# A fused attention and expert layer on one core: alibi transfers issued by GpSimd, a reordered prologue, and the last head's masks, gates and sums moved

## The chip, the core and the metric

The kernel runs on one core of a Trainium2 chip. The metric is the device time of one execution in microseconds, the median of several runs. Engines are TensorE (PE in the rows; PEld is its weight load), VectorE (DVE), ScalarE (ACT), GpSimd (POOL) and SyncE (SP). Each works through its own list in order and waits at semaphores. SyncE and GpSimd also issue DMA transfers, GpSimd with descriptors that it writes itself (the software queue of the profile).

## The reference

The input x is 2 sequences of 1024 rows of 256 values. With xn = layernorm(x), the output is x + s * g, where s is causal attention and g = silu(f) of an expert layer:

```python
scores = einsum('bhqd,bhkd->bhqk', q, k) * SCALE + rel * alibi_slopes   # 16 heads of 16, S = 1024
scores = where(causal_mask, -inf, scores)
attn = maximum(softmax(scores), 1e-10)
s = (attn @ v) @ out_w.T + out_b
probs = softmax(rmsnorm(xn) @ w_router)        # 32 experts, 4 per token, capacity 128
f = xn + sum of chosen experts + sigmoid(...) * shared expert (width 704)
return x + s * silu(f)
```

## The kernel before

All semaphores are set by hand, and each engine's list is written out in `build`. A *unit* is one head of one sequence, together with one expert: 32 units. Phase k of a unit loop works on pass 2 of head k, pass 1 of head k+2, the values of head k-1 and expert k+2, so the engines are interleaved; phases -2 to 1 and the last ones are unrolled, the rest is a loop (`phases`).

**Prologue.** VectorE normalises sixteen tiles (line 1296) and computes slope rows for alibi (1316). TensorE transposes them, makes queries and keys (`qk`, 724), router logits (690), transposes of the RMS-normalised rows (674 again), counts and places the tokens' choices (701, 712), values (747, 735), column sums (756, 762). ScalarE copies each block of queries or keys twice out of PSUM (1083, 1084) and splits it with VectorE into three bf16 parts (1071, 1335, 1328), in a ring of four buffers `SPL`; block i waits until block i-4 is stored. SyncE stores the parts (`store_parts`, 488) to `q_parts` and `k_parts`, writes the alibi rows of the stacked operands (`store_alibi`, 470 to 480, ten transfers for each sequence), stores the RMS-normalised rows to `xf_rows` (503), and loads from the parts the stacks of 111 rows that the score products use (`load_stack`, 516 and 518). The alibi sources lie in `VS`, where the values go later, and the normalised rows lie in `STACKS`, so `VS` may be written only after all alibi transfers, and a stack may be loaded only after `xf_rows` is stored. Its queue in order: moe_rows, alibi of sequence 0, parts 0 to 7, alibi of sequence 1, xf_rows, stack 0, part 8, half of stack 1, part 9, the other half, parts 10 to 15, the router table (552), stacks 2 and 3, four experts. VectorE, behind its routing work, places choices (`place`, 1390) among parts 12 to 15, finishes the table for the gathers (1407 to 1413) and evacuates every other group of values (1431). GpSimd splits the bias rows (1656 to 1660) at once, waits for the normalised rows, and splits the shared expert's weights (1719, 1720).

**A unit.** Pass 1 (`pass1`) makes scores of a query tile, with a mask product of 128 columns (784) in front, VectorE takes the row maximum (1440), ScalarE the exponential with row sum (1126). GpSimd turns sums into shifts (`chain`). Pass 2 (`pass2`) makes transposed scores, ScalarE takes the exponential (1135), VectorE clamps it (1446), GpSimd sets the masked half of the diagonal tiles to zero (`fill_diagonal`, 1670), TensorE multiplies with the values (`values`, 838, 841) and VectorE evacuates the head (1499).

**The end.** The sums of the expert rows come back by eight loads (633); ScalarE takes tanh of each (`tanh_sum`, 1194), VectorE makes the gate (1508) and, for the eighth block, first adds the shared expert (`last_sum`, 1515). In phase 31 these stand between the clamps of the last head. Blocks 0 to 3 are multiplied early (1521) and added to the output by GpSimd's accumulating transfers (1826). Blocks 4 to 7 need the last head: two of its four stores are issued by SyncE (597), two by ScalarE (1257); then project (935), multiply (1528), add x (1537), store (644).

## Time and profile before

| | us |
|---|---|
| median of 3 runs (604.64 to 607.84) | 606.28 |
| the profiled execution | 604.26 |
| its span, first to last instruction | 602.4 |
| TensorE busy in the span | 542.0 (90%) |
| VectorE busy | 467.1 (78%) |
| ScalarE busy | 455.9 (76%) |
| GpSimd busy | 313.1 (52%) |
| share of TensorE in the chain that ended last | 74% |
| first score product starts | 116.67 |

The page has shares over the whole span. This kernel has three stages with different limits (prologue to 116.67, the unit loop, the output), so the stages are read by the chain in order of time, the waits, and the instructions in order of time. In a row of the last kind the bracket is the idle time of the engine in front of it and who ended it.

### The profile page before, as it was taken

Reading aid. Unit: us, or ns where it says so; the run is one execution under the profiler, and the core shown is the slowest. Engines: PE = TensorE matmul, PEld = TensorE weight load, DVE = VectorE, ACT = ScalarE, POOL = GpSimd, SP = SyncE. Lnnn points to the kernel's source line nnn. Section 1 sums busy time; section 2 is a strip of 40 time slices with the busy share of each in tenths; the row PEclk is TensorE's granted clock in tenths of the full one; section 3 lists DMA queues with packets and bytes.
Section 4 is the critical chain, followed back from the end, with each engine's and each line's share of the span. In section 5 each row is a group of like instructions: output and inputs, shape, how many; then the busy total and the mean of one; then the engine's idle time right before and its main releaser. Section 6 shows DMA issues by size and latency. Waiting matters only on the chain.

```text
span 602.4 us, 16652 instructions
## 1 busy us (share of the span) xinstructions
PE 542.0 (90%) x4359; PEld 368.5 (61%) x4360; DVE 467.1 (78%) x1065; ACT 455.9 (76%) x1061; POOL 313.1 (52%) x696
## 2 busy tenths in 40 slices
PE   0897918788999999999999999999999999999954
PEld 0566416665666667666666666666666666766733
DVE  5969939368778968986897799689868977996356
ACT  1639523268889979997998899799979988997650
POOL 7780000325656566556756565665566655754431
PEclk9997966989999999999999999999999999999988
DMA  8786845713435335443643353354335444542338
GB/s 242 244 149 177 183 158 151 193 46 65 100 92 119 95 88 122 102 107 79 142 110 94 88 127 90 89 114 104 100 84 131 119 100 124 118 107 62 83 101 142
DMA packets 74321, 71.44 MB, mean 119 GB/s; under 512 B 12787, under 2 KB 64693, under 8 KB 74165
## 3 DMA queue, kind: packets, MB, share of 16 engines
q1 hardware_dynamic: 65076, 59.28, 35.3%
q0 software_dynamic: 9136, 11.80, 13.1%
q8 instruction: 12, 0.20, 0.2%
q14 instruction: 17, 0.13, 0.1%
q10 hardware_dynamic: 80, 0.03, 0.0%
HBM read 47.82 MB, written 23.59 MB: 119 GB/s over the span
## 4 chain that ended last, share of the span: by engine, by line
PE 74%; DVE 8%; DMA 7%; SPq 4%; ACT 3%; issue 2%; POOL 1%; POOLq 0%; DVEq 0%; ACTq 0%
PE PSB L816 11%; PE PSB L917 11%; PE PSB L788 10%; PE PSB L925 7%; PE PSB L838 6%; PE PSB L878 6%; PE PSB L841 5%; PE PSB L784 5%; PE PSB L896 4%; PE PSB L747 2%; SPq L476 2%; DMA xf_rows<-STACKS 2%; PE PSB L889 2%; DMA q_parts<-PB 2%; DMA XN<-in_L_attn_qkv_dram 1%
## 5 line engine op out<-in xcount | busy, mean ns | idle before, releaser
L1440 DVE TENSOR_REDUCE NEGM<-PSB 128x1 f32<-128x1024 f32 (+7 forms) x256 | 189.8, 752 | 60.8 <-PE PSB L788 58.2
L1135 ACT ACTIVATE PB<-PSB 128x128 f32<-128x128 f32 (+7 forms) x256 | 166.0, 649 | 37.9 <-PE PSB L816 34.6
L1126 ACT ACTIVATE PSB<-PSB,NEGM 128x1024 f32<-128x1024 f32 (+7 forms) x256 | 183.2, 716 | 11.1 <-DVE NEGM L1440 7.8
L1446 DVE TENSOR_SCALAR PB<-PB 128x128 f32<-128x128 f32 (+7 forms) x256 | 110.3, 468 | 10.0 <-ACT PB L1135 9.9
L816 PE MATMUL PSB<-STACKS 111*128 111x512 bf16 (+3 forms) x384 | 104.3, 327 | 2.9 <-ACT PB L1135 0.3
L788 PE MATMUL PSB<-STACKS 111*128 111x512 bf16 (+3 forms) x384 | 101.8, 328 | 0.0
L1781 POOL DMA_INDIRECT moe_rows<-YE,IDX x32 | 55.7, 1739 | 28.6 <-issue 28.6
L838 PE MATMUL PSB<-PB,VH 128*32 128x256 f32 x640 | 69.2, 389 | 0.0
L1670 POOL TENSOR_SCALAR_AFFINE_SELECT PB<-PB 128x512 f32<-128x512 f32 x64 | 42.0, 657 | 42.5 <-DVE PB L1446 42.5
L841 PE MATMUL PSB<-PB,VH 128*32 128x128 f32 x1024 | 57.0, 280 | 7.3 <-POOL PB L1670 6.6
L784 PE MATMUL PSB<-MQ,IDB 128*128 128x128 bf16 x256 | 55.8, 224 | 6.3 <-ACT PSB L1126 5.6
L1741 POOL COPY IDX<-TABS 128x2 int32 (+1 forms) x32 | 25.3, 790 | 66.2 <-DVE TABS L1413 65.2
L816 PEld LDWEIGHTS PSB<-STACKS 111*128 111x128 bf16 x384 | 31.5, 97 | 43.8 <-ACT PB L1135 25.9
L841 PEld LDWEIGHTS PSB<-PB,VH 128*32 128x32 f32 x1024 | 48.0, 111 | 12.2 <-issue 9.6
L1745 POOL DMA_INDIRECT XES<-xf_rows,IDX x32 | 38.2, 1193 | 32.7 <-POOL IDX L1741 29.9
L1126 ACT ACTIVATION_READ_ACCUMULATOR PSB<-PSB,NEGM 128x1 f32 x256 | 51.6, 202 | 0.0
L784 PEld LDWEIGHTS PSB<-MQ,IDB 128*128 128x128 bf16 x256 | 24.5, 96 | 42.7 <-ACT PSB L1126 19.5
L925 PE MATMUL PSB<-SWD,HS 128*128 128x256 f32 x192 | 48.5, 387 | 0.0
L878 PE MATMUL PSB<-WGU,XES 128*128 128x352 f32 x128 | 48.0, 458 | 0.0
L838 PEld LDWEIGHTS PSB<-PB,VH 128*32 128x32 f32 x640 | 34.6, 111 | 11.2 <-issue 11.1
L925 PEld LDWEIGHTS PSB<-SWD,HS 128*128 128x128 f32 x192 | 34.4, 189 | 9.3 <-issue 5.3
L788 PEld LDWEIGHTS PSB<-STACKS 111*128 111x128 bf16 x384 | 32.6, 98 | 10.3 <-issue 6.0
(201 smaller groups left out, 1097.4 us busy)
## 6 DMA issues: line engine op xcount, KB each, us to landing
WGU<-in_L_ffn_w_gate_dram SPq DMA_DIRECT2D x32, 176.0 KB
WGU<-in_L_ffn_w_up_dram SPq DMA_DIRECT2D x32, 176.0 KB
WDS<-in_L_ffn_w_down_dram SPq DMA_DIRECT2D x32, 176.0 KB
q_parts<-PB SPq DMA_DIRECT2D x8, 384.0 KB, 3.6
STACKS<-q_parts SPq DMA_DIRECT2D x32, 96.0 KB
STACKS<-k_parts SPq DMA_DIRECT2D x32, 96.0 KB
XN<-in_L_attn_qkv_dram SPq DMA_DIRECT2D x4, 512.0 KB, 6.0
moe_rows<-XN SPq DMA_DIRECT2D x1, 2048.0 KB, 7.5
```

The lines of the kernel that those rows point to most:

```text
L784: pe.matmul(psf[:, base + i * P:base + w], IDB[:, :], MQ[:, :], start=True, stop=False, skip_group_check=True)
L788: ins = pe.matmul(psf[:, base + c0:base + c1], q, KS[slot][0:ROWS, c0:c1], start=(c1 < w), stop=True, skip_group_check=True)
L816: ins = pe.matmul(psf[:, base + c0:base + c1], key, QS[slot][0:ROWS, j * P + c0:j * P + c1], start=(c0 > 0 or not masked), stop=True, skip ...
L838: ins = pe.matmul(o, v, probs[:, c - j:far - j + 1:far - c, :], start=False, stop=(j == 0), skip_group_check=True)
L841: ins = pe.matmul(o[:, 1, :], v, probs[:, far - j, :], start=(far == j), stop=False, skip_group_check=True)
L878: ins = pe.matmul(o[:, 0:2 * F], XET[:, part, :], WGU[slot][:, part, :], start=(part == 0), stop=(part == KC - 1))
L917: ins = pe.matmul(o[0:m, part * BLK:(part + 1) * BLK], w[:, c, ch * P:ch * P + m], v[:, c, :], start=(c == 0 and v is XFH and w is high), ...
L925: ins = pe.matmul(o[:, 0:D], HS[0:m, ch, which * P:(which + 1) * P], SWD[0:m, ch, :], start=(ch == 0), stop=(ch == NF - 1))
L1126: act.activation(sc, sc, ACT.Exp, bias=NEGM[:, par, i:i + 1], accum_out=LSUM[:, par, i:i + 1]).then_inc(exp1_done, 1)
L1135: act.activation(PB[:, k % 2, prob_offset(s):prob_offset(s) + (s + 1) * P], psf[:, base:base + (s + 1) * P], ACT.Exp).then_inc(exp2_done, 1)
L1440: dve.tensor_reduce(NEGM[:, par, i:i + 1], psf[:, base:base + (i + 1) * P], AX_X, ALU.max, negate=True).then_inc(max_ready, 1)
L1446: dve.tensor_scalar(p, p, FLOOR, 0.0, ALU.subtract, ALU.max).then_inc(clamp_done, 1)
```

## The change

- `store_alibi` moves from SyncE to GpSimd's queue, both sequences in a row, behind the bias split and ahead of the split of the shared weights. GpSimd waits for all normalised tiles before the bias split instead of after it.
- SyncE's queue becomes: moe_rows, parts 0 to 7, xf_rows, parts 8 to 11, a wait for all alibi transfers, stack 0, parts 12 and 13, stack 1, parts 14 and 15, then as before.
- The first value group and the choices' counts swap PSUM banks; placing products go to value groups 3, 5, 7 and behind the last; all eight value groups are evacuated by ScalarE.
- In the last head every tile of pass 2 gets a mask product; its fills go, and its values wait for seven clamps instead.
- VectorE's gates 1 to 3 and early products 0 and 1 go behind the last head's last clamp, the last sum, early products 2 and 3 and gates 4 to 6 behind the last evacuation. Of the late blocks, GpSimd adds x to 4 and 5, VectorE to 6 and 7.

```diff
...
-W0, XN0, QK0, R0, XF0, QK1, POS0, V0, U0 = 0, 4, 12, 20, 22, 30, 38, 39, 47
+W0, XN0, QK0, R0, XF0, QK1, V0, POS0, U0 = 0, 4, 12, 20, 22, 30, 38, 39, 47
+def v_task(g):
+    return V0 + g + (g > 0)
...
@@ sync
-            def store_alibi(b):
...
-            sp.wait_ge(slope_rows_ready, 1)
-            sp.wait_ge(int_rows_ready, 5)
-            store_alibi(0)
             for n in range(8):
                 store_parts(n)
-            sp.wait_ge(alibi_stored, 16 * 10)
-            store_alibi(1)
             sp.wait_ge(xf_ready, NT)
...
             sp.dma_start(rows_t[:, :, 0:D], XF).then_inc(xf_stored, 16)
-            sp.wait_ge(xf_stored, 16)
-            for n in range(XF0, XF0 + 8):
-                sp.wait_ge(pro_free[n % 8], n // 8 + 1)
...
+            for n in range(8, 12):
+                store_parts(n)
+            sp.wait_ge(xf_stored, 16)
+            for n in range(XF0, XF0 + 8):
+                sp.wait_ge(pro_free[n % 8], n // 8 + 1)
+            sp.wait_ge(alibi_stored, 16 * 10 * B)
             load_stack(0, 0, 0)
-            store_parts(8)
-            load_queries(DH, 1, 1)
-            store_parts(9)
-            load_keys(DH, 1, 1)
-            for n in range(10, 16):
-                store_parts(n)
+            store_parts(12)
+            store_parts(13)
+            load_stack(DH, 1, 1)
+            store_parts(14)
+            store_parts(15)
...
-                sp.wait_ge(fin_out, g - NT // 4 + 1)
+                if g < NT // 4 + 2:
+                    sp.wait_ge(fin_added, g - NT // 4 + 1)
+                else:
+                    sp.wait_ge(fin_out, g - NT // 4 - 1)
@@ tensor
-                for h in {1: (0, 1), 3: (2,), 5: (3,)}.get(g, ()):
+                for h in {3: (0,), 5: (1,), 7: (2,)}.get(g, ()):
                     place_choices(h)
...
+            place_choices(3)
...
-                masked = s == NQ - 1
+                masked = s == NQ - 1 or is_last(it, k)
...
-                if batch == 0:
+                if batch == 0 and not is_last(it, k):
                     pe.wait_ge(fill_done, unit(it, k, len(FILLED), len(FILLED)))
+                elif batch == 0:
+                    pe.wait_ge(clamp_done, unit(it, k, NQ, VALUE_BATCH[0][-1] + 1))
@@ scalar
-            for g in range(0, 8, 2):
+            for g in range(8):
...
@@ vector
-            dve.wait_ge(alibi_stored, 16 * 10 * B)
-            for g in range(1, 8, 2):
-                n = V0 + g
-                dve.wait_ge(pro_ready[n % 8], n // 8 + 1)
-                dve.tensor_copy(values_of(g), products_of(n)).then_inc(pro_free[n % 8], 1)
...
                     if isinstance(it, int) and k == UNITS and s == 0:
+                        for g in range(1, 4):
+                            gate(g)
                         for g in range(2):
                             early_product(g)
+                    if isinstance(it, int) and k == UNITS and s == 3:
+                        last_sum()
+                        for g in range(2, NT // 4):
+                            early_product(g)
+                        for g in range(NT // 4, NT // 2 - 1):
+                            gate(g)
                     if here:
                         clamp(it, k, s)
-                    if isinstance(it, int) and k == UNITS - 1 and s >= 2:
-                        if s == 3:
-                            last_sum()
-                        else:
-                            gate((0, 0, 1, 2, 3)[s - 2])
+                    if isinstance(it, int) and k == UNITS - 1 and s == 2:
+                        gate(0)
...
-            for g in range(2, NT // 4):
-                early_product(g)
-            for g in range(NT // 4, NT // 2):
-                gate(g)
+            gate(NT // 2 - 1)
             for g in range(NT // 4, NT // 2):
                 product(g)
+            for g in range(NT // 4 + 2, NT // 2):
                 add_input(g)
@@ gpsimd
+            pool.wait_ge(xn_ready, NT)
             pool.wait_ge(row_loaded, 64)
...
-            pool.wait_ge(xn_ready, NT)
...
+            pool.wait_ge(slope_rows_ready, 1)
+            pool.wait_ge(int_rows_ready, 5)
+            store_alibi(0)
+            store_alibi(1)
             pool.wait_ge(sw_loaded, 16 * 10)
...
-                if exists(it, k):
+                if exists(it, k) and not is_last(it, k):
                     fill_diagonal(it, k, 0)
...
+            pool.wait_ge(x_again[1], 32)
+            for g in range(NT // 4, NT // 4 + 2):
+                n = g - NT // 4
+                x_late = XAGAIN[:, 512 * n:512 * (n + 1)]
+                pool.wait_ge(fin_product, n + 1)
+                pool.tensor_tensor(x_late, x_late, TANH[g], ALU.add).then_inc(fin_added, 1)
```

## Rows read from the trace of the kernel before

**Rows 1.** Chain that ended last, in order of time: start us, us, what.

```profile
39.96 4.80 DMA q_parts<-PB
64.17 10.88 DMA xf_rows<-STACKS
80.01 4.58 DMA q_parts<-PB
```

**Rows 2.** Waits of 0 to 100 us: engine, tile, line, for whom; us, times, longest.

```profile
ACT PB L1083 <- DMA q_parts<-PB: 23.0, 3, 13.4
```

**Rows 3.** Line 476: count, issue ns min/median/max, first and last start.

```profile
L476 SPq DMA_DIRECT2D q_alibi<-VS x8: 353/655/924, 32.1 to 61.3; - x8
```

**Rows 4.** VectorE in order of time: start, us, line, names; last its idle time.

```profile
33.98 0.67 DVE L1328 TENSOR_TENSOR PB<-PB 128x512 bf16<-128x512 f32 x1
...
54.82 0.76 DVE L1348 TENSOR_TENSOR HS<-PSB,NR 128x264 f32<-128x264 f32 x2
...
66.59 1.28 DVE L1335 TENSOR_TENSOR PB<-PB 128x512 f32<-128x512 f32 x2
...
67.97 0.69 DVE L1328 TENSOR_TENSOR PB<-PB 128x512 bf16<-128x512 f32 x1
...
86.09 0.69 DVE L1335 TENSOR_TENSOR PB<-PB 128x512 f32<-128x512 f32 x1 [9.42 <-ACT PB L1084]
...
99.17 5.29 DVE L1390 TENSOR_SCALAR WDS<-IOC,PK 128x128 bf16<-128x128 bf16 x32
...
107.03 0.19 DVE L1407 COPY DUMP<-PSB 128x32 f32<-128x32 f32 x1 [2.58 <-PE PSB L712]
```

**Rows 5.** TensorE in order of time, prologue and first expert.

```profile
49.27 0.83 PE L690 MATMUL PSB<-RW,XNT 128*128 128x33 f32 x3
...
106.37 0.63 PE L712 MATMUL PSB<-PB,WDS 128*128 128x64 bf16 x16
...
112.76 0.95 PE L756 MATMUL PSB<-TS,WIT 128*128 128x2 f32 x8
...
116.67 0.22 PE L784 MATMUL PSB<-MQ,IDB 128*128 128x128 bf16 x1 [0.51 <-ACT UL L1113]
...
125.00 1.35 PE L878 MATMUL PSB<-WGU,XES 128*128 128x352 f32 x4
```

**Rows 6.** A window: length; busy PE, PEld, DVE, ACT, POOL; clock, DMA.

```profile
25.00:50.00 25.00, 24.52 (x97) 16.89 (x98) 17.80 (x38) 11.91 (x21) 17.52 (x15) 0.85 0.81 191
```

**Rows 7.** VectorE in order of time, last head and output.

```profile
579.05 0.69 DVE L1515 TENSOR_TENSOR XFT<-XFT,XNT 128x512 f32<-128x512 f32 x1 [3.77 <-DMA XFT<-moe_rows]
...
589.11 0.48 DVE L1499 TENSOR_SCALAR OEV<-PSB,UL 128x256 f32<-128x256 f32 x1 [4.36 <-PE PSB L838]
...
593.30 0.69 DVE L1528 SCALAR_TENSOR_TENSOR VS<-PSB,XFT 128x512 f32<-128x512 f32 x1
...
598.28 0.69 DVE L1537 TENSOR_TENSOR XNT<-XNT,VS 128x512 f32<-128x512 f32 x1
```

**Rows 8.** TensorE, then ScalarE, in order of time, same stretch.

```profile
585.28 0.65 PE L841 MATMUL PSB<-PB,VH 128*32 128x128 f32 x8 [6.64 <-POOL PB L1670]
...
578.44 1.03 ACT L1135 ACTIVATE PB<-PSB 128x1024 f32<-128x1024 f32 x1
...
589.62 1.57 ACTq L1257 DMA_DIRECT2D XN<-OEV  x2
```

**Rows 9.** Line 1296 in 15 to 20 and 21.8 to 24.2 us: ns min/median/max.

```profile
L1296 DVE TENSOR_SCALAR XN<-XN,MV,NRM x5: 691/745/1315, 15.8 to 19.6; 128x256 f32<-128x256 f32 x5
...
L1296 DVE TENSOR_SCALAR XN<-XN,MV,NRM x7: 400/402/404, 21.5 to 23.4; 128x256 f32<-128x256 f32 x7
```

**Rows 10.** Line 488, all its sixteen issues: us from issue to landing.

```profile
DMA to landing us min/median/max: 2.5/3.2/5.9
```

**Rows 11.** GpSimd: two transfers in order of time; line 1720, ns min/median/max.

```profile
590.49 2.44 POOL L1826 DMA_DIRECT2D out_dram<-WDS  x2 [2.83 <-DVE WDS L1521]
...
L1720 POOL TENSOR_TENSOR SWUL<-WGU,SWUH x4: 924/956/8367, 30.2 to 42.2; 128x352 fp32r<-128x352 f32 x4
```

More of the change, by code:

```diff
@@ L1653, in _, with store_alibi @@
                       allow_small_or_imprecise_dtypes=True).then_inc(const_ready, 1)
+            def store_alibi(b):
+                qa = q_alibi[b * H:(b + 1) * H, 3:15].rearrange("h (p r) s -> h p r s", r=4)
+                ka = k_alibi[b * H:(b + 1) * H, 3:15].rearrange("h (p r) s -> h p r s", r=4)
+                for dst, r, src in ((qa, 0, None), (qa, 2, None), (ka, 1, None), (ka, 3, None),
+                                    (ka, 0, 0), (ka, 2, 1), (qa, 1, 2), (qa, 3, 3)):
+                    source = SROW if src is None else \
+                        IROW[:, src:src + 1, :].broadcast_to([H, 3, S])
+                    pool.dma_start(dst[:, :, r, :], source).then_inc(alibi_stored, 16)
+                pool.dma_start(k_alibi[b * H:(b + 1) * H, 0:3], ONER.unsqueeze(1).broadcast_to([H, 3, S]))\
+                    .then_inc(alibi_stored, 16)
+                pool.dma_start(q_alibi[b * H:(b + 1) * H, 0:3], ZROW.unsqueeze(1).broadcast_to([H, 3, S]))\
+                    .then_inc(alibi_stored, 16)
+            pool.wait_ge(xn_ready, NT)
             pool.wait_ge(row_loaded, 64)
@@ L1791, in _ @@
             copy_block(0, 0)
-            for n in range(V0, V0 + 8):
+            for g in range(8):
+                n = v_task(g)
                 pool.wait_ge(pro_free[n % 8], n // 8 + 1)
@@ L1816, in phase @@
                     copy_block(it, w + 1)
-                if exists(it, k):
+                if exists(it, k) and not is_last(it, k):
                     fill_diagonal(it, k, 1)
```

21 lines of the change are left out of this document (6 added, 15 removed).

## The prediction

> **What bounds the kernel now.** I read the page first. TensorE carries most of the chain that ended last, and that is the repeated work on the heads, which the change leaves as it is. So only the two ends are of interest: the prologue before the first score product, and the last head with the output.
>
> The chain in order of time shows the prologue. Three transfers issued by SyncE carry it: the store of the first split part at 39.96, the store of xf_rows at 64.17 (10.88 us) and the store of part 8 at 80.01 [rows 1]. The waits say who stands behind them: ScalarE waited 23.0 us in three pieces for stored parts, 13.4 the longest [rows 2]. Parts go through four buffers, so ScalarE cannot write part i before part i-4 has landed. What delayed the stores was SyncE's queue: the twenty alibi transfers, 0.35 to 0.92 us of issue each, from 32.1 to 61.3 [rows 3], in two lots, the first ahead of part 0 and the second ahead of xf_rows; then the eight transfers of stack 0 ahead of part 8. Behind ScalarE VectorE stood still until 86.09, 9.42 us of it in one piece [rows 4]; TensorE then waited for VectorE's placements and began the first score product only at 116.67 [rows 5].
>
> At the end VectorE waits 3.77 us at 579.05 for the last sum's load, with clamps queued behind it; gates and clamps alternate; the fill on GpSimd is late and TensorE starts the last head's values at 585.28, 6.64 us idle [rows 7, 8].
>
> **The change, part by part.** *Bias split behind the normalisation.* While GpSimd splits the bias, VectorE's normalising instructions take 745 ns (median of five); later they take 402 [rows 9]. Sixteen run from 15.8 to 23.8, 8.0 us; at 0.402 they take 6.4: **-1.6 us**. TensorE is busy 24.52 of the 25 us from 25 to 50 [rows 6], so the end of the router products, 50.10 [rows 5], moves by the same to 48.5.
>
> *Alibi transfers on GpSimd.* SyncE now stores part 0 when its split ends: 34.65 less 1.6 is 33.05 [rows 4]; with 0.4 of issue and 3.2 to land (2.5 to 5.9, [rows 10]) ScalarE gets its buffer back at 36.7 and not at 44.8. From there to VectorE's scaling of the logits at 54.82 took 10.0 us, which gives 46.7 (49.4 with the slowest landing); the router products end at 48.5, later. The second scaling, 55.2 before, is due at 48.6: **-6.6 us** in all so far. TensorE's router products are late next, so part of the 8 us stays hidden. From 54.82 to 66.59 VectorE works without a wait [rows 4]; that is kept, and so are the 10.1 us from there to 76.67, where its long wait began. It reaches that point at 70.1.
>
> *Parts 8 to 11 ahead of stack 0.* Part 8 was split at 68.66 [rows 4], 62.1 now; issued and landed it is there at 65.7 (68.4 at worst), ScalarE's two copies take some 1.4, so VectorE finds its next operand by 70.1: the whole 9.42 us go, **-16.0 us** so far. From 86.09 to 99.17 VectorE is nearly full; kept, it ends at 83.2. Two placements of 5.29 together [rows 4] end at 88.5.
>
> *Order of value products and placements.* Before, VectorE ended its placements at 104.5 and TensorE worked off value products until 112.76 [rows 4, 5]. Now seven of eight value groups run while VectorE is still placing, and behind the last placement stand one product group of 0.63 [rows 5] and three reads of 0.19 [rows 4], with hand-overs some 1.4 us: the column-sum product of 112.76 is due at 89.9, **-22.8 us**. The 3.91 us from there to 116.67 stay: first score product at 93.9. The four evacuations that VectorE loses to ScalarE lie beside this, since ScalarE has no other work there.
>
> *What the moved transfers meet on GpSimd's queue.* The slope rows are ready at 30.5 (32.1 before). Two DMA instructions issued at 590.49, beside dense two-input work on VectorE, took 2.44 us [rows 11]: 1.2 each, 24 us for twenty, the last landed near 60. SyncE asks for them at about 72, ScalarE about then too. Behind them on GpSimd comes the split of the shared weights, eight subtractions of 0.96 [rows 11] and eight casts, taken at half: some 12 us, wanted by SyncE's expert loads only at 96. Both have over 10 us of cover. Beside VectorE's dense stretch one GpSimd subtraction took 8.37 us [rows 11]; that much on one or two of them still fits.
>
> The split now lies beside VectorE's full stretch. Bounds: nothing (the stretch of that 8.37) and 12 us, if each GpSimd instruction holds VectorE for its length, as in [rows 9]. I take **+1.0**, near the dense row, because most of VectorE's work there is of that kind. SyncE: a stack took 4.9 us of issue [rows 1]; stacks 1 to 3, from about 80, and the parts and table between them end near 96, the first expert's three loads near 97.5, landed at 101 to 103.4; its product came 8.33 us after the first score product [rows 5], 102.2 now. **+0.5**, bounds 0 and 3.
>
> The Trainium skill speaks against this part: DMA: Bandwidth & Descriptors, section Issuing engines are not separate DMA queues, says that issuing from several engines saves only the sequencer's issue time, usually small beside the transfer. By it the alibi move gives almost nothing, a rival below; here [rows 2, 3] show that issue time and its order is what ScalarE waits for.
>
> *The last head.* Masks added by seven more 128-column products replace the fill: 0.22 us each [rows 5], overlapped by their neighbours; bounds 0 and 1.5, taken 0.4. The last exponential ends at 579.5 [rows 8], 579.9 now, and the last clamp, no longer behind gates and the awaited sum, at 580.6. TensorE starts the values after the clamp before, no later than 579.5, and is done by 583.3 even at the 3.83 us that it took before (585.28 to 589.11, [rows 7, 8]). VectorE does three gates and two early products first, 0.69 each as in [rows 7]: the evacuation falls at 584.1 instead of 589.11. ScalarE's two head stores now wait for the moved last sum and its tanh, 0.69 and about as much: behind the evacuation's 0.48 they start at 586.0 and not at 589.62 [rows 8], only 3.6 earlier. From that issue to the first late product 3.68 us passed [rows 7, 8]: 589.7. VectorE's seven remaining steps end near 589.4, so it is just ready. Eight steps from 593.30 to 598.97 become six, 4.25 us, ending at 593.95; GpSimd's two sums take 1.35 each (0.93 for 352 columns, [rows 11]) and end by 593.1. The 3.43 us from the last sum to the end of the span stay: 597.4, **-5.0 us** (bounds -3.5, if GpSimd's sums are held off until VectorE is idle, and -6.5, if the stores come sooner).
>
> **Sum.** -22.8 + 1.0 + 0.5 - 5.0 = -26.3 us. The profiled execution took 604.26 us (span 602.4), so 578.0; it lies 2.0 under the median of 606.28, so the median is forecast at **580.0 us**.
>
> **The rivals.** *VectorE pays for GpSimd.* Each instruction of the weight split holds VectorE, as bias and normalisation held each other [rows 9]: 10.5 more than I took on the chain that starts at 48.6, 590.5. For it: that chain has no slack. Against it: the dense row.
>
> *GpSimd starves (slower).* If VectorE keeps GpSimd from writing its descriptors, SyncE gets its stacks late: after the last issue come 5 us to land, four stacks of 4.9 and 6 for the first expert, 31 in all. The first expert product came at 125.0 [rows 5]; with the tail's 5.0 the break-even is at 130.0, so the last issue at 99, which is 3.4 us for each transfer against 1.2 in [rows 11]. At 5 us each they end at 130.5 and the kernel comes to about 637. Against it: [rows 11], and that VectorE's gaps would let some through.
>
> The Trainium skill states such a rule: SBUF — State Buffer, section SBUF: two separate sides, has descriptors written by GpSimd blocked while VectorE runs a two-port instruction, with 620 ns growing to 3100. Five times 1.2 would be 6 us each. The trace does not bear it out for two-input work [rows 11]; VectorE's work beside the transfers is mostly of that kind.
>
> *Issue time was not the wait.* Stored parts stay late for their bytes: only the normalisation's 1.6 and the tail's 5.0 remain, 599.7. Against it: landing takes 3.2 us [rows 10], the longest wait 13.4 [rows 2].
>
> *The ends come late.* The first expert by 3 us, GpSimd's sums held, landings at their slowest: together +5, 585.0.
>
> **How the numbers follow.** Forecast 0.71; ends late 0.11; VectorE pays 0.11; issue time 0.03; starving 0.04. On the fast side stand no port cost, no expert wait and the full tail, 2.9 us less, and the 1.6 by which the fastest of the three runs lies under their median: 575. For 8 in 10 the range reaches from 575 to 591, up to the port rival. About 0.5% is what a measurement of this kernel tells from no change. Faster 0.95; same 0.01; slower 0.04.
>
> **What would show it.** First score product near 94, no ScalarE wait of over 3 us for a stored part, VectorE without a gap from 48 to 88, alibi transfers of some 1.2 us each landed by 60; last evacuation near 584, last output issue near 594. Wrong it would be by VectorE's steps stretched between 50 and 75, by TensorE waiting for an expert or a gather behind 98, or by a loop whose period changed.

## The result and the profile after

| | before | after |
|---|---|---|
| median of 6 runs each, us | 606.25 (603.35 to 607.84) | 601.47 (599.36 to 602.92) |
| ratio after to before, 95% interval | | 0.9932 (0.9907 to 0.9956) |
| span of the profiled execution, us | 602.4 | 600.7 |
| first score product starts | 116.67 | 104.76 |
| first head evacuated | 158.99 | 154.88 |
| head 30 (the last but one) evacuated | 574.47 | 574.73 |
| last head evacuated | 589.11 | 583.61 |

The kernel is 0.7% faster, not 4.3%; 580.0 was forecast, and 601.5 lies outside 575 to 591. The table shows where the gain went, by the two profiled spans (1.7 us apart; the medians are 4.8 apart). The prologue gained 11.9 us up to the first score product. The stretch from there to the first evacuation gave 7.8 back (50.1 us, 42.3 before). The loop gave back 4.4 (419.9 us from the first head to head 30, 415.5 before). The end gained 2.0 (26.0 us behind head 30, 27.9 before). -11.9 + 7.8 + 4.4 - 2.0 = -1.7. The profiled execution of the kernel before lies 2.0 under its median, that of the changed kernel 0.9 over it, so this account covers 1.7 of the 4.8 us. The evacuations of the first head and of head 30, before:

```profile
158.99 0.47 DVE L1499 TENSOR_SCALAR OEV<-PSB,UL 128x256 f32<-128x256 f32 x1
...
574.47 0.48 DVE L1499 TENSOR_SCALAR OEV<-PSB,UL 128x256 f32<-128x256 f32 x1
```

and after:

```profile
154.88 0.47 DVE L1488 TENSOR_SCALAR OEV<-PSB,UL 128x256 f32<-128x256 f32 x1
...
574.73 0.48 DVE L1488 TENSOR_SCALAR OEV<-PSB,UL 128x256 f32<-128x256 f32 x1
```

**Prologue.** GpSimd in order of time (start, us, line, names; in brackets the idle time before). The first and last of ten rows with the twenty alibi transfers:

```profile
26.88 1.27 POOL L1655 DMA_DIRECT2D q_alibi<-VS  x2 [2.00 <-DVE VS L1311]
...
36.70 0.51 POOL L1658 DMA_DIRECT2D q_alibi<-HS  x1
```

They are issued in 10.3 us, 0.5 each. ScalarE behind them, its first copy of a block (line 1077, 1083 before) into a buffer that must have been stored:

```profile
36.52 0.69 ACT L1077 ACTIVATE PB<-PSB,BQS 128x512 f32<-128x512 f32 x1 [5.25 <-DMA q_parts<-PB]
...
44.74 0.69 ACT L1077 ACTIVATE PB<-PSB,BQS 128x512 f32<-128x512 f32 x1 [6.43 <-DMA q_parts<-PB]
...
53.42 0.69 ACT L1077 ACTIVATE PB<-PSB,BQS 128x512 f32<-128x512 f32 x1 [6.90 <-DMA k_parts<-PB]
```

That is 18.6 us of waiting for stored parts, where [rows 2] had 23.0. Part 0 is issued at 29.2 (39.96 before, [rows 1]), but the chain that ended last now has the landing of part 2 in it, and the sixteen stores of line 480 land late:

```profile
33.18 20.14 DMA k_parts<-PB
...
114.28 4.35 issue
```

```profile
DMA to landing us min/median/max: 2.5/4.2/20.1
```

[Rows 10] had 2.5/3.2/5.9. A window beside it (length; busy PE, PEld, DVE, ACT, POOL; clock, DMA share, GB/s) shows the sixteen DMA engines full while few bytes move:

```profile
40.00:50.00 10.00, 7.57 (x47) 7.16 (x46) 5.72 (x7) 1.78 (x3) 9.52 (x13) 0.62 0.99 125
```

VectorE then scales the logits, and TensorE starts its column sums and the first score product; the first expert's product comes 13.9 us behind that, at half clock, behind the wait of 4.35 us that the chain shows too:

```profile
59.39 0.77 DVE L1343 TENSOR_TENSOR HS<-PSB,NR 128x264 f32<-128x264 f32 x2
```

```profile
100.64 1.05 PE L748 MATMUL PSB<-TS,WIT 128*128 128x2 f32 x8 [0.73 <-DVE TABS L1405]
...
104.76 0.26 PE L776 MATMUL PSB<-MQ,IDB 128*128 128x128 bf16 x1 [0.51 <-ACT UL L1108]
...
118.63 2.69 PE L872 MATMUL PSB<-WGU,XES 128*128 128x352 f32 x4 [4.35 <-issue]
```

**Loop.** A turn of four units takes 55.6 us before, in each of seven; after, five take 56.3 to 56.4, one 55.6 and one 56.0. GpSimd in two turns of the changed kernel, a short one and a long one: scatter, copy of scales (line 1772), second fill (1676), seed of the chain (1686).

```profile
227.53 1.65 POOL L1791 DMA_INDIRECT moe_rows<-YE,IDX  x1 [0.89 <-issue]
...
232.37 0.18 POOL L1772 COPY SGB<-SG 128x2 f32 x1
...
234.05 0.69 POOL L1676 TENSOR_SCALAR_AFFINE_SELECT PB<-PB 128x384 f32<-128x384 f32 x1
234.83 0.20 POOL L1686 TENSOR_SCALAR LNS<-LSUM 128x8 f32<-128x8 int32 x1
...
283.11 1.84 POOL L1791 DMA_INDIRECT moe_rows<-YE,IDX  x1 [0.90 <-issue]
...
288.28 1.15 POOL L1772 COPY SGB<-SG 128x2 f32 x1
...
290.22 1.03 POOL L1676 TENSOR_SCALAR_AFFINE_SELECT PB<-PB 128x384 f32<-128x384 f32 x1
291.34 0.52 POOL L1686 TENSOR_SCALAR LNS<-LSUM 128x8 f32<-128x8 int32 x1
```

VectorE beside the long one:

```profile
288.31 1.08 DVE L1435 TENSOR_SCALAR PB<-PB 128x768 f32<-128x768 f32 x2
...
290.81 0.99 DVE L1435 TENSOR_SCALAR PB<-PB 128x1024 f32<-128x1024 f32 x1
```

The copy of two columns meets two clamps and ends with them (289.4); the fill behind it meets the next clamp, the seed comes 0.9 us late against the scatter, and ScalarE waits 1.02 us for it. In the short turn the copy is done ahead of the clamps. Before, the copy takes 0.17 us in each of the seven turns.

**End.** VectorE, GpSimd's four accumulating transfers, ScalarE's two head stores, TensorE's late projections, VectorE's last sums and SyncE's four output stores, in order of time:

```profile
582.40 1.29 DVE L1510 TENSOR_TENSOR WDS<-STACKS,XFT 128x512 f32<-128x512 f32 x2
583.61 0.48 DVE L1488 TENSOR_SCALAR OEV<-PSB,UL 128x256 f32<-128x256 f32 x1
583.68 5.05 POOL L1837 DMA_DIRECT2D out_dram<-WDS  x4 [14.75 <-DVE WDS L1510]
...
584.72 1.62 ACTq L1252 DMA_DIRECT2D XN<-OEV  x2
...
589.29 6.71 PE L929 MATMUL PSB<-OWT,XN 128*128 128x256 f32 x16 [6.52 <-DMA XN<-OEV]
591.37 0.69 DVE L1517 SCALAR_TENSOR_TENSOR VS<-PSB,XFT 128x512 f32<-128x512 f32 x1 [3.08 <-PE PSB L929]
...
593.50 4.84 SPq L635 DMA_DIRECT2D out_dram<-XNT  x4
...
596.65 1.28 DVE L1526 TENSOR_TENSOR XNT<-XNT,VS 128x512 f32<-128x512 f32 x2
```

From the last evacuation to the end 17.1 us pass, 13.3 before: ScalarE's stores start 1.11 behind it (0.51 in [rows 7, 8]) and, in the chain, land in 4.43 us (2.40); TensorE, idle for 6.52 us, has a granted clock of 0.50 (1.2 GHz) from 589 to 592, and its sixteen projections take 6.71 us (3.69).

This end is not the same in every execution. The same code for the end stands in six more of the kernels below, and there 24.1 to 25.2 us pass from head 30 to the end (26.0 here), with sixteen projections of 5.41 to 6.43 us; the old end took 27.2 to 28.8 in three kernels (27.9 before). The new end thus gains about 3 us by the means (24.9 against 28.0), and the 2.0 of the table is this one execution's. Differences of less than 2 us between the ends of two single executions cannot be read.

### The profile page after: what moved, and what is told of

The parts are those of the page before. It is cut to its first block, busy times and chain, and to the rows that moved or that the text cites. A ratio compares the mean times of both kernels' runs of the same rounds, so it can differ in the third digit from the quotient of the medians.

```text
span 600.7 us, 16661 instructions
## 1 busy us (share of the span) xinstructions
PE 544.8 (91%) x4366; PEld 369.1 (61%) x4367; DVE 464.8 (77%) x1059; ACT 457.2 (76%) x1065; POOL 322.3 (54%) x716
## 4 chain that ended last, share of the span: by engine, by line
PE 57%; DVE 11%; issue 9%; DMA 9%; ACT 7%; POOL 6%; POOLq 1%; SPq 0%; ACTq 0%; DVEq 0%
PE PSB L808 9%; PE PSB L919 7%; PE PSB L911 7%; PE PSB L780 7%; PE PSB L872 5%; PE PSB L832 4%; ACT PSB L1121 4%; PE PSB L890 3%; DMA moe_rows<-YE,IDX 3%; DMA k_parts<-PB 3%; PE PSB L835 3%; PE PSB L776 3%; PE PSB L929 2%; ACT PB L1130 2%; DVE WDS L1385 1%
## 5 line engine op out<-in xcount | busy, mean ns | idle before, releaser
L1435 DVE TENSOR_SCALAR PB<-PB 128x128 f32<-128x128 f32 (+7 forms) x256 | 112.4, 475 | 12.9 <-ACT PB L1130 12.7
L832 PE MATMUL PSB<-PB,VH 128*32 128x256 f32 x640 | 67.8, 384 | 0.0
L776 PE MATMUL PSB<-MQ,IDB 128*128 128x128 bf16 x256 | 56.4, 226 | 7.0 <-ACT PSB L1121 6.3
L808 PEld LDWEIGHTS PSB<-STACKS 111*128 111x128 bf16 x384 | 31.5, 97 | 44.6 <-ACT PB L1130 26.1
L835 PE MATMUL PSB<-PB,VH 128*32 128x128 f32 x1024 | 55.5, 276 | 1.2 <-DVE PB L1435 0.2
L1676 POOL TENSOR_SCALAR_AFFINE_SELECT PB<-PB 128x512 f32<-128x512 f32 (+1 forms) x62 | 39.9, 643 | 30.7 <-DVE PB L1435 30.7
L1751 POOL COPY IDX<-TABS 128x2 int32 (+1 forms) x32 | 26.8, 836 | 52.3 <-DMA xf_rows<-PB 52.3
L872 PE MATMUL PSB<-WGU,XES 128*128 128x352 f32 x128 | 49.4, 470 | 4.3 <-issue 4.3
L835 PEld LDWEIGHTS PSB<-PB,VH 128*32 128x32 f32 x1024 | 47.1, 109 | 6.3 <-issue 2.9
L1454 DVE SCALAR_TENSOR_TENSOR RT<-ET,PSB 128x256 f32<-128x256 f32 (+2 forms) x80 | 30.4, 380 | 15.9 <-ACT ET L1150 11.7
L832 PEld LDWEIGHTS PSB<-PB,VH 128*32 128x32 f32 x640 | 33.7, 109 | 10.6 <-issue 10.4
```

The lines of the kernel that those rows point to most:

```text
L776: pe.matmul(psf[:, base + i * P:base + w], IDB[:, :], MQ[:, :], start=True, stop=False, skip_group_check=True)
L808: ins = pe.matmul(psf[:, base + c0:base + c1], key, QS[slot][0:ROWS, j * P + c0:j * P + c1], start=(c0 > 0 or not masked), stop=True, skip ...
L832: ins = pe.matmul(o, v, probs[:, c - j:far - j + 1:far - c, :], start=False, stop=(j == 0), skip_group_check=True)
L835: ins = pe.matmul(o[:, 1, :], v, probs[:, far - j, :], start=(far == j), stop=False, skip_group_check=True)
L872: ins = pe.matmul(o[:, 0:2 * F], XET[:, part, :], WGU[slot][:, part, :], start=(part == 0), stop=(part == KC - 1))
L1435: dve.tensor_scalar(p, p, FLOOR, 0.0, ALU.subtract, ALU.max).then_inc(clamp_done, 1)
```

## The experiments

Each ratio is to the kernel before, run on the same chip beside it. The changed kernel's own is 0.9932.

**The two halves.** One kernel has the last head and the output as before, the other is the kernel before with the new ones.

```diff
-                masked = s == NQ - 1 or is_last(it, k)
+                masked = s == NQ - 1
... (prologue alone: with this every line of the change on the last head, gates, sums; tail alone: these lines only)
```

> The changed kernel with the last head and the output as before; it tells what the new prologue is worth by itself, and whether the longer loop period of the changed kernel (56.3 us for four units, 55.6 before) comes with the prologue. Theory "the loop's period hangs on which GpSimd instructions meet VectorE's clamps": the period is 56.3 or so in most turns, the 4.1 us by which the first head was ahead are gone at head 28, and the time is about 606, no change. Rival "the period comes from the changed tail's code": period 55.6, lead kept, about 602.

> The kernel before with the changed last head and output alone. As I forecast it: last evacuation 5 us earlier and the end 5.0 earlier, 601.2. Rival "the output takes it back" (head stores land in 4.4 us instead of 2.4 beside four accumulating transfers, and the sixteen last projections run at the lower clock, 6.7 us for 3.7): last evacuation 5 us earlier, end only 1.7 earlier, 604.5. Loop period 55.6 by both.

Prologue alone 0.9978 (0.9955 to 1.0000), tail alone 0.9949 (0.9925 to 0.9973). The prologue alone has its first head at 155.19, 3.8 us ahead, and head 30 at 572.35, 2.1 ahead, so 1.7 of the 3.8 are lost: it has two long turns where the changed kernel has five, and the time fell between the two I had named. The tail alone has its last head at 584.49, 4.6 earlier, and a span of 599.7, 2.7 less than before; this, too, lies between the theories, and 0.8 of it went to a long turn. It has one long turn of 56.4 (the copy at 180.64 took 1.16) with the prologue as before: so long turns belong to neither half in particular.

**Alibi transfers later.** Theory: they keep the DMA engines busy, whoever issues them. Rival: parts are late for their own bytes.

```diff
@@ gpsimd, ahead of the split of the weights
-            pool.wait_ge(slope_rows_ready, 1)
-            pool.wait_ge(int_rows_ready, 5)
-            store_alibi(0)
-            store_alibi(1)
...
@@ gpsimd, behind it
+            for r in range(RING):
+                pool.wait_ge(split_stored[r], 32)
+            pool.wait_ge(slope_rows_ready, 1)
+            pool.wait_ge(int_rows_ready, 5)
+            store_alibi(0)
+            store_alibi(1)
```

> The changed kernel with the twenty alibi transfers behind GpSimd's weight split and behind the landing of parts 0 to 7. Theory "the alibi transfers keep the DMA engines busy, whoever issues them, and stored parts land late beside them": parts 0 to 3 land in about 3 us, ScalarE waits under 3 us for a part before 50, the logits' second scaling is at about 50 instead of 59.4, the xf_rows store or parts 8 to 11 land later instead, and the first score product comes at 96 to 100 instead of 104.8; the whole gains 2 to 8 us: 593 to 599. Rival "parts are late for their own bytes, or for ScalarE's and VectorE's own work beside GpSimd's split": landing stays over 10 us or the waits move to other reasons, scaling at 59, and 601 to 603.

0.9886 (0.9853 to 0.9920). The logits are scaled at 46.70, 12.7 us earlier, parts 0 to 7 land 2.5 to 2.7 us after their issue, and ScalarE waits at most 0.6 us for parts 0 to 3. The landing of line 480 becomes

```profile
DMA to landing us min/median/max: 2.5/3.6/17.9
```

and the chain shows the long one beside the transfers' new place (57 to 68):

```profile
63.53 17.61 DMA q_parts<-PB
```

The theory holds: the stall moved with the transfers, from parts 0 to 2 to parts 8 and 9, for which ScalarE waits 8.32 and 6.21 us. So the first score product gains 1.1 us only (103.65), which misses the 96 to 100 that I expected of it, and the first head 0.7. Most of what this span is shorter (3.7 us) came elsewhere: 2.2 in the loop, which has three long turns here, and 0.8 behind head 30. Windows say what is scarce: with parts alone, then with the xf_rows store, then with the alibi transfers on.

```profile
33.00:47.00 14.00, 14.00 (x83) 12.09 (x82) 14.00 (x29) 11.78 (x21) 14.00 (x1) 0.82 0.54 185
50.00:56.00 6.00, 6.00 (x19) 2.81 (x17) 5.90 (x26) 5.95 (x12) 5.55 (x5) 1.00 0.89 297
...
66.00:80.00 14.00, 7.66 (x46) 6.16 (x45) 7.64 (x20) 2.42 (x5) 1.82 (x4) 0.86 1.01 145
```

The engines are busier at 145 GB/s with the alibi rows than at 297 without: a byte of that mix costs 2.3 times the engine time. (The alibi rows are 1.9 MB, read from sixteen partitions; that this is the reason is not shown by any run here.)

**Half of them gone.** The second sequence's rows equal the first's, and are copied in DRAM later.

```diff
@@ gpsimd
             store_alibi(0)
-            store_alibi(1)
... (the waits for all twenty become waits for ten; the loop waits for the copies)
@@ sync, behind the first four experts
+            for rows in (q_alibi, k_alibi):
+                sp.dma_start(rows[H:2 * H], rows[0:H]).then_inc(alibi_copied, 16)
```

> The changed kernel with ten of the twenty alibi transfers gone from GpSimd's burst: the second sequence's rows, which are the same, are copied from the first's inside DRAM by two transfers of SyncE behind the first four experts. Theory "the alibi transfers keep the DMA engines busy and stored parts land late beside them": with half the burst the waits of ScalarE for parts 0 to 3 (18.6 us in the changed kernel) fall to 6 to 11 us, the scaling of the logits comes at 50 to 54 instead of 59.4, no part behind them waits over 5 us, and the first score product comes at 94 to 99 instead of 104.8; the whole gains 4 to 9 us less what the first expert then waits. Rival "parts are late for their own bytes": waits as before, scaling at 59, no gain.

0.9800 (0.9751 to 0.9849), against 0.9932 about 8 us. Logits scaled at 52.61, two waits for parts of 9.0 us together, first score product at 99.49 (half a microsecond outside what I expected), first head at 148.89:

```profile
52.61 0.76 DVE L1348 TENSOR_TENSOR HS<-PSB,NR 128x264 f32<-128x264 f32 x2
```

By the profiled spans, 10.8 us apart, 6.0 were gained up to the first head, 3.4 in the loop (one long turn instead of five) and 1.4 behind head 30. Fewer transfers, not another issuer, shorten the prologue.

**The move by itself.** The kernel before with its alibi transfers on GpSimd and the wait for them ahead of stack 0.

```diff
@@ sync
-            store_alibi(0)
...
-            sp.wait_ge(alibi_stored, 16 * 10)
-            store_alibi(1)
...
+            sp.wait_ge(alibi_stored, 16 * 10 * B)
             load_stack(0, 0, 0)
@@ gpsimd
...
+            store_alibi(0)
+            store_alibi(1)
```

> The kernel before with the alibi transfers alone moved to GpSimd's queue (with the wait for all twenty ahead of stack 0); all else as before. As I forecast it (issue time in SyncE's queue was what ScalarE waited for): logits scaled at 48 to 50 instead of 54.8, 5 to 7 us gained. Theory "the DMA engines are the limit": parts 0 to 2 are issued early and land late, logits scaled at 58 to 60, first score product within 3 us of 116.7, the whole within 0.5% of the kernel before.

1.0013 (0.9991 to 1.0035). The logits are scaled at 62.00, later than in either kernel and 2 us later than the theory had it; the first score product comes at 114.02, and the landing of the parts has the same row as in the changed kernel, 2.5/4.2/20.1. By the ratio the move is worth nothing; the profiled execution, 602.10, is the fastest of ten (the others took 604.63 to 607.58), so its 2.7 us at the first score product may not stand for the rest.

**Experts ahead of stacks 2 and 3.**

```diff
-            for u in (2, 3):
-                load_stack(u * DH, u, u)
             sp.wait_ge(sw_split, 2 * SLOTS)
             sp.wait_ge(place_free, 4)
-            for u in range(4):
-                load_expert(u, u)
+            for u in range(2):
+                load_expert(u, u)
+            for u in (2, 3):
+                load_stack(u * DH, u, u)
+            for u in (2, 3):
+                load_expert(u, u)
```

> The changed kernel with the loads of experts 0 and 1 issued by SyncE ahead of stacks 2 and 3; nothing else differs. Theory "the sixteen transfers of stacks 2 and 3, 97.1 to 110.5, hold the first expert, for which TensorE waits 4.35 us at 114.3": experts issued from about 101, first expert product at 114 to 115 instead of 118.6, first head's evacuation 3 to 4 us earlier, the whole 3 to 4 us shorter. Rival "the loads are bound by the DMA engines or by stacks 2 and 3 that then come late": the wait moves to the third head, evacuations of heads 2 and 3 as before, gain under 1 us.

0.9810 (0.9772 to 0.9848), and the first head at 149.54, 5.3 us earlier, more than I expected, though the first score product was 1.6 later (106.39). From that product to the first head it takes 43.1 us, 50.1 in the changed kernel and 42.3 before. (Another 2.0 us of its span were gained in the loop, with three long turns, and 0.8 behind head 30.) The first expert's product follows without a wait and takes half as long:

```profile
115.69 1.35 PE L874 MATMUL PSB<-WGU,XES 128*128 128x352 f32 x4
```

So SyncE's queue was the cause: in the changed kernel the sixteen transfers of stacks 2 and 3 hold it from 97.1 to 110.5, the first and the last row here,

```profile
97.13 5.35 SPq L499 DMA_DIRECT2D STACKS<-q_parts  x3
...
110.04 0.41 SPq L501 DMA_DIRECT2D STACKS<-k_alibi  x1
```

and TensorE did not wait for those stacks when they were issued 7 us later. The wait also cost clock: the four products took 2.69 us behind it.

**The scales' copy one unit later.**

```diff
-                if exists(it, w) and w % SLOTS == 0:
-                    copy_scales(it, w)
+                if exists(it, w) and w % SLOTS == 1:
+                    copy_scales(it, w - 1)
```

> The changed kernel with the copy of two columns of scales (128x2) moved in GpSimd's list by one unit, out of the unit where it takes 1.15 us beside a clamp of VectorE; nothing else differs. Theory "the longer period is this copy, and the fill and the seed behind it, held by VectorE": the fill takes 0.65 and the seed 0.2 us in that unit, period 55.6 and not 56.3, seven turns, 4 to 5 us: about 597. Rival "the period is longer because the scatter's additions land late": the copy is short but the period stays 56.3, 601.5.

0.9910 (0.9875 to 0.9945), and all seven turns take 55.5 to 55.6. In the unit in question the scatter is as long as in the long turn above, and the fill and the seed are short all the same:

```profile
283.96 1.85 POOL L1791 DMA_INDIRECT moe_rows<-YE,IDX  x1 [0.90 <-issue]
...
290.42 0.69 POOL L1676 TENSOR_SCALAR_AFFINE_SELECT PB<-PB 128x384 f32<-128x384 f32 x1
291.20 0.19 POOL L1686 TENSOR_SCALAR LNS<-LSUM 128x8 f32<-128x8 int32 x1
```

The copy was the hinge, not the scatter. From the first head to head 30 it takes 415.4 us, as before. The profiled span is 4.0 us shorter than the changed kernel's (4.4 in the loop and 1.3 behind head 30 gained, 1.7 lost up to the first head); by the ratios the gain is 1.3 us, their intervals overlap, and about 597 us was expected. So the loop's 4.4 us stand on the turns, not on the whole time. The turns of all the kernels run here bear it out: where the copy takes 0.17 to 0.20 us, a turn takes 55.5 to 55.7; where it takes 1.15 to 1.28, 56.2 to 56.4; where it was moved it takes 0.51 to 0.53, and every turn 55.5 to 55.7.

**The end, three ways.** Accumulating transfers held until the head's rows have landed; TensorE kept busy in the wait; the sums on VectorE again.

```diff
@@ gpsimd (held)
+            for c in range(4):
+                pool.wait_ge(last_rows[c], 16)
@@ tensor (kept busy)
+                    for n in range(20):
+                        pe.matmul(PSB[:, 0, 0:D], OWT[:, 0, 0:P], OWT[:, 1, :], start=True, stop=True)
@@ vector (sums)
             for g in range(NT // 4, NT // 2):
                 product(g)
-            for g in range(NT // 4 + 2, NT // 2):
                 add_input(g)
... (GpSimd's two sums and SyncE's waits for them go)
```

> The changed kernel with the four accumulating output transfers of GpSimd held until the last head's rows have landed; nothing else differs. Theory "the last head's stores land late beside these transfers, 4.4 us instead of 2.4": the four stores land in about 2.4 us, the first late projection starts about 2 us earlier (587.3 by the times of the changed kernel), and the end is 2 us earlier, up to 5 if TensorE's clock then stays up. Rival "the transfers only move, and delay GpSimd's two sums or the late output instead": the projections start earlier, the end does not move or comes later.

> The changed kernel with twenty products of 128x256 added on TensorE behind the last head's values, into a bank that nobody reads; they fill its wait for the last head's rows and add nothing to the output. Theory "TensorE's clock has fallen in that wait (granted 0.50 from 589 to 592), and the sixteen late projections take 6.7 us for that": the clock stays at 1.0, they take 3.7, the end comes 2.5 to 3 us earlier. Rival "the end is set by the landing of the output and by VectorE's and GpSimd's last steps": projections 3.7 us, end less than 1 us earlier.

> The changed kernel with all four late sums on VectorE again, as before; it prices the sums on two engines. As I forecast it (two steps of 0.69 us less on VectorE): this kernel's end comes 1.4 us after that of the changed one, 0.2% slower. Rival "with TensorE's clock down the projections, 1.7 us each pair, set the pace and VectorE has time for the sums": its last sum ends no later than the changed kernel's, under 0.5 us of difference in the span behind the last evacuation.

Held: 0.9980 (0.9959 to 1.0001), slower than the changed kernel. The projections start 3.5 us behind the evacuation (582.29) instead of 5.7, but GpSimd's two sums now stand behind its transfers and take as long as these, the clock had fallen anyway, and from head 30 to the end 28.3 us pass, outside the 24.1 to 26.0 of the unchanged end:

```profile
585.76 6.26 PE L929 MATMUL PSB<-OWT,XN 128*128 128x256 f32 x16 [4.30 <-DMA XN<-OEV]
...
590.00 4.93 POOL L1846 TENSOR_TENSOR XNT<-XNT,VS 128x512 f32<-128x512 f32 x2
```

Kept busy: 0.9950 (0.9930 to 0.9971). The sixteen projections take 3.62 us, but the span ends 16.7 us behind the evacuation instead of 17.1:

```profile
580.13 8.80 PE L956 MATMUL PSB<-OWT 128*128 128x256 f32 x40
588.76 3.62 PE L929 MATMUL PSB<-OWT,XN 128*128 128x256 f32 x16
```

The rival holds: the clock's 3 us are not the end's 3 us (25.6 us behind head 30, inside the range of the unchanged end). Sums on VectorE: 0.9938 (0.9920 to 0.9955), the end 16.5 us behind the evacuation and 25.5 behind head 30, inside that range too.

Its last sum, from 597.32 to 598.01, ends 13.9 us behind the evacuation, the changed kernel's 14.3. The sixteen projections take 6.65 us there, as slow as the changed kernel's; those of one late block take 1.7, so VectorE has time for the sum between them: on two engines the sums are worth nothing here.

**The three edits together,** half the transfers, experts first, scales later.

> The changed kernel with three of the tried edits together: half the alibi transfers, experts 0 and 1 ahead of stacks 2 and 3, the scales' copy one unit later. If the three costs are separate places on one chain, the first score product is at 98 to 100, TensorE has no wait of over 2 us for the first expert, the first head's evacuation is at 144 to 147 (154.9 in the changed kernel), the loop's period is 55.6 in every turn, and the ratio to the kernel before is 0.970 to 0.978. If the first expert is then held by something else (the router table's store, the gather), evacuation at 148 to 149 and about 0.978 to 0.982.

583.32 us, 0.9646 (0.9621 to 0.9671), better than I expected, and close to the sum of the three: against 0.9932 they gave 0.0132, 0.0122 and 0.0022 by themselves, 0.0286 together. First score product at 97.55, first expert without a wait at 106.87, first head at 140.74, 14.1 us ahead of the changed kernel, and no long turn:

```profile
106.87 1.35 PE L879 MATMUL PSB<-WGU,XES 128*128 128x352 f32 x4
```

**And the evacuation early.** In the changed kernel TensorE is done with the last values at 581.5, and VectorE evacuates them at 583.61, behind three gates and two products. On top of the three edits:

```diff
@@ vector, last head
-                        for g in range(1, 4):
-                            gate(g)
-                        for g in range(2):
-                            early_product(g)
...
-                        for g in range(2, NT // 4):
+                        for g in range(NT // 4):
                             early_product(g)
...
-                    if isinstance(it, int) and k == UNITS - 1 and s == 2:
-                        gate(0)
+                    if isinstance(it, int) and k == UNITS - 1 and s in (2, 3, 5, 6):
+                        gate((0, 1, 1, 2, 3)[s - 2])
@@ scalar: the two head stores ahead of tanh_sum(NT // 2 - 1)
```

> The kernel with the three edits together, and in the last head VectorE's gates 1 to 3 back between the clamps, early products 0 and 1 behind the evacuation, and ScalarE's two head stores ahead of the last tanh. In the changed kernel TensorE is done with the last values at 581.5, VectorE evacuates them at 583.6, behind three gates and two products, and the accumulating transfers then start ahead of the head's stores. Theory "the tail loses by the late evacuation and by the transfers that go ahead of the head's rows": from the last loop head's evacuation to the last one 6.7 to 7.2 us instead of 8.9, ScalarE's stores 0.5 us behind it, landed in 2.4 to 3 us, end 2 to 5 us earlier than in the kernel with the three edits, ratio to the kernel before 0.957 to 0.962. Rival "VectorE's own steps behind the last clamp, some 14 of 0.65 us, set the end whatever their order": evacuation earlier, end less than 1 us earlier, 0.963 to 0.966.

581.79 us, 0.9612 (0.9585 to 0.9639); its interval and that of the three edits overlap. The evacuation comes 2.0 us earlier against head 30 (6.8 instead of 8.9 behind it), the end 1.6 (22.8 instead of 24.4 in the kernel with the three edits, and outside the 24.1 to 26.0 of the unchanged end): less than the theory wanted, more than the rival. What gates, products and stores gave each was not run. Its end:

```profile
564.11 0.48 DVE L1495 TENSOR_SCALAR OEV<-PSB,UL 128x256 f32<-128x256 f32 x1 [0.86 <-PE PSB L839]
...
564.62 1.58 ACTq L1258 DMA_DIRECT2D XN<-OEV  x2
...
566.91 3.69 PE L936 MATMUL PSB<-OWT,XN 128*128 128x256 f32 x16 [1.58 <-DMA XN<-OEV]
...
569.92 2.48 DVE L1524 SCALAR_TENSOR_TENSOR VS<-PSB,XFT 128x512 f32<-128x512 f32 x4
...
572.76 2.76 SPq L642 DMA_DIRECT2D out_dram<-XNT  x4
```

The stores go ahead of the accumulating transfers (566.38) and have landed 2.3 us after their issue; TensorE is idle for 1.58 us and keeps its clock. Now VectorE is late, its first product stands behind ten other steps; its last step still ends 17.8 us behind head 30, 3.9 us earlier than with the three edits alone (21.7), but the end comes 5.0 us behind that instead of 2.7: what is late next is the landing of the output (a median of 3.6 us for SyncE's four stores, 2.2 with the three edits).

## Why the prediction was wrong, step by step

Between the forecast (-26.3 us) and the two profiled spans (-1.7) lie 24.6 us: 10.9 of them in the prologue, 6.3 at the first expert (7.8 lost where +0.5 and +1.0 were taken), 4.4 in the loop, 3.0 at the end.

**Bias behind the normalisation (-1.6):** right in kind, too small. The sixteen tiles are normalised from 14.45 to 19.71, 0.33 us each, and are done 4.1 us earlier than before (23.82): 2.8 by shorter steps, 1.3 by an earlier start. The durations in [rows 9] overlap, so sixteen times 0.402 was too long. Behind the late parts the extra 2.5 us did not show; with the alibi transfers later the scaling came at 46.70.

**Alibi on GpSimd, "with 0.4 of issue and 3.2 to land": the step that failed.** The prediction took the landing of a part (2.5 to 5.9, [rows 10]) as it was with the alibi transfers in the same queue, where part 0 came behind ten of them, and let part 0 go beside them. Issue times came out better than foreseen (0.51 us for each transfer, not 1.2), and that was the harm: twenty transfers reached the DMA engines in one burst with parts 0 to 3, which landed 7.2 to 20.1 us after their issue. ScalarE waited 18.6 us for parts, where no wait of over 3 us was expected. The second scaling of the logits came at about 59.8 (two of 0.4 us from 59.39 on), not at 48.6: 11.2 us of the 22.8 gone. The experiments with the transfers later, halved and moved alone show it. The rival *Issue time was not the wait*, given 0.03, was right that issue time was not the wait, but not in its reason: without the alibi transfers beside them the parts landed in 2.5 to 2.7 us, so they are not late for their own bytes. That its time came near (599.7 for 601.5) is luck: it kept 1.6 us of the prologue and the tail's 5.0, where the profiles show gains of 11.9 and 2.0, and 12.2 lost between. The Trainium skill, DMA: Bandwidth & Descriptors, section Issuing engines are not separate DMA queues, had been cited against this part: transfers of all issuers run on the same sixteen engines. The trace agrees with it, with 1.0013 for the move alone. The profile before had it too: from 35 to 40 us, with the first ten transfers on SyncE's queue, its DMA engines were busy at 0.93 with 102 GB/s; I had looked at the wait and the issue, not at that ([rows 6] has 0.81 with 191 for the whole stretch):

```profile
35.00:40.00 5.00, 5.00 (x19) 2.61 (x17) 4.44 (x10) 1.71 (x3) 5.00 (x1) 1.00 0.93 102
```

**Parts 8 to 11 ahead of stack 0; the order of values and placements:** right. From the second scaling of the logits to the first score product I had 45.3 us (48.6 to 93.9); it took 45.0. The wait of 9.42 us [rows 4] is gone.

**GpSimd and VectorE at one port (+1.0):** not met as forecast. With the parts late, the weight split fell beside stretches in which VectorE waited for ScalarE; there VectorE's two-input steps took 1.37 instead of 0.67 us, ahead of the next wait. Where VectorE was dense, with the transfers later, GpSimd was the one that waited: one cast took 16.64 us. Neither the rival in which VectorE pays nor the one in which GpSimd starves decided anything. (The price of the first should read 11.0, 12 less the 1.0 taken, not 10.5.)

**First expert (+0.5, bounds 0 to 3): mis-sized.** 7.8 us were lost between the first score product and the first head. The order of SyncE's queue was known, stacks 2 and 3 ahead of the experts, and I placed them by a prologue that ran 11 us earlier; with the parts late these stacks were issued only from 97.1 on, and the product moved only 6.4 us earlier while the score products moved 11.9. The experiment with experts first gives back 7.0 of the 7.8.

**Loop unchanged: failed,** taken at nothing in the sum, though named as what would prove it wrong. It cost 4.4 us in the profiled execution. The copy of the scales meets VectorE's clamps or not; the experiment with the copy moved, with turns as before, shows that this is all of it. What decides in a given turn is open. From 240 to 286 us of the kernel before, TensorE, ScalarE and VectorE of the two kernels run at a distance of 3.34 to 3.36 us; then the scatter starts 0.03 us later in the changed one, the index copy behind it takes 1.07 us instead of 0.76, and the copy of the scales comes 0.35 us later against the rest. Why the index copy took longer is not shown. Long turns were found in all kernels but the one before and those with the copy moved; how many an execution has may well vary, and one profile for each kernel can't tell.

**Tail (-5.0): the evacuation right, the end wrong.** 583.61 for 584.1; the end gained 2.0 in this execution and about 3 by all the traces, instead of 5.0. Three terms were taken as in [rows 7, 8], out of a stretch where other things ran. From the stores to the first late product I had 3.68 us; it took 6.65, beside the accumulating transfers, which the earlier products had set free in the same microsecond. The projections stood behind a wait that had grown from 1.84 to 6.52 us, ran at a granted clock of 0.50 at first and took 6.71 us instead of 3.69. And two steps less on VectorE are worth nothing as long as TensorE sets the pace. Of the single cures none moved the end out of the range that the unchanged end has in other executions, but for the held transfers, which made it later; the earlier evacuation with the stores ahead did, and the landing of the output was late next. So the three terms are seen in the traces, but what each is worth in the end's time stays open.

## What to carry to other kernels

Before a transfer is moved to another issuer, look at the share of the DMA engines' time beside the bytes in its stretch: if they are full, as here (0.93 with 102 GB/s), the transfers have to become fewer or go where the engines are idle; a queue that issued faster made its neighbours later (up to 20.1 us to land). When a stage becomes earlier, go through the queue behind it for what keeps its place (here sixteen loads ahead of the first expert), and at an output put the few small stores that others wait for ahead of the large ones that nobody does. A sum that takes the loop as unchanged needs a look at how close a GpSimd instruction lies to VectorE's long ones; the sign in a trace is one instruction with two durations (here 0.18 and 1.15 us) in different turns. And before an end of a few microseconds is compared between two executions, see how much it varies where its code is the same (here by 2 us).

## What the runs showed of the hardware

- A transfer of 96 KB took 0.51 us of issue on GpSimd's queue (the first two 0.64 each), beside two-input work on VectorE up to 33.9 us; [rows 11] had 1.2 for 256 KB, and the four of the output still took 1.26 each.
- Stores of 384 KB issued on SyncE's queue while such transfers run landed in 7.2 to 20.1 us, in 2.5 to 2.7 without (parts 0 to 7 with the transfers later); the DMA engines were busy at 0.99 then with 125 GB/s, and reached 297 GB/s at 0.89 with other stores.
- A GpSimd copy of 128x2 took 1.15 us where it met two clamps of VectorE (288.28 and 288.31, both through at 289.4) and 0.18 where it did not; with what stood behind it, that lengthened a turn of four units by 0.7 to 0.8 us. The Trainium skill, SBUF — State Buffer, section SBUF: two separate sides, has the two engines hold their shared port in turn, each for a whole instruction, the first to start first. That the copy ends with the clamps agrees. Which of the two was first the trace cannot tell: by it the copy, which waited, starts 0.03 us earlier, and its spans on GpSimd are rough.
- TensorE's granted clock was 0.50 (1.2 of 2.4 GHz) behind an idle stretch of 6.52 us and behind one of 4.30 us, and 1.0 behind one of 1.58 us. The first expert's four products took 2.69 us at a granted clock of 0.50 (118.6 to 121.3), behind the wait of 4.35 us, and 1.35 at 1.00 (115.7 to 117.0) without it.
